# A third place in PSUM for the turned cross-attention exponents of a decoder layer

## What is computed

```
x = x + self_attn(layernorm(x))                 # 16 heads of 32: 6 plain, 4 hyperbolic, 6 cosine
x = x + cross_attn(layernorm(x), ctx)           # 16 heads, 224 queries, 750 keys per batch, mask
x = x + peer_ffn(layernorm(x))                  # product keys, 8 heads x top 8 of 128*128 experts

# cross_attn, per batch and head (d = 32):
att = (q @ k.T) / sqrt(d)                       # 224 x 750
att = att * mask - 1e10 * (1 - mask)
att = softmax(att)
out = att @ v                                   # 224 x 32, then @ Wo + bo
```

## Time and profile before

| what | value |
| --- | --- |
| median of 3 runs | 2667.64 us (2662.12, 3053.95, 2667.64) |
| the profiled execution's own time | 2672.23 us |
| its span, first to last instruction | 2670.4 us |
| PE busy | 2355.7 us, 88% |
| DVE busy | 1870.6 us, 70% |
| ACT busy | 1185.9 us, 44% |
| POOL busy | 1122.6 us, 42% |

### The profile page before, as it was taken

How to read it: one execution, slowest core, us unless ns; L and a number is a source line. 1 busy time by engine, 2 the same in 40 slices (tenths; PEclk the granted TensorE clock), 3 DMA queues, 4 the chain that set the end, 5 groups by cost and what they waited for, 6 DMA issues and landing times. The chain is left out here.

```text
span 2670.4 us, 37760 instructions
## 1 busy us (share of the span) xinstructions
PE 2355.7 (88%) x12440; PEld 1263.5 (47%) x12440; DVE 1870.6 (70%) x5466; ACT 1185.9 (44%) x3230; POOL 1122.6 (42%) x1084
## 2 busy tenths in 40 slices
PE   7899999999999999999777799898989898897777
PEld 3455564555655556555554344444444344443322
DVE  3477676776768667677554896878878787878555
ACT  1447365573745737466351343343334333433322
POOL 2121111211112111121001676777777777777775
PEclk9899999999999999999878899999999999999999
DMA  5000101001010010100202998999999999999998
GB/s 179 8 24 8 37 2 30 16 8 38 1 45 1 8 38 1 45 1 22 93 1 85 372 391 335 399 401 418 395 416 397 410 409 399 400 395 395 407 416 355
DMA packets 161362, 520.73 MB, mean 195 GB/s; under 512 B 17168, under 2 KB 27408, under 8 KB 161168
## 3 DMA queue, kind: packets, MB, share of 16 engines
q0 software_dynamic: 129024, 469.82, 44.3%
q1 hardware_dynamic: 30560, 46.98, 5.3%
q10 hardware_dynamic: 1584, 1.52, 0.2%
HBM read 507.71 MB, written 10.55 MB: 194 GB/s over the span
## 5 line engine op out<-in xcount | busy, mean ns | idle before, releaser
L1593 POOL DMA_INDIRECT e_rows<-in_experts,e_idx x896 | 888.2, 991 | 340.9 <-issue 287.7
L1650 PE MATMUL e_ps_out<-e_rows,e_diag 128*128 128x512 f32 x1792 | 843.5, 617 | 145.3 <-ACT e_diag L1917 145.1
L1811 DVE CUSTOM_DVE_ANT_0 e_rows<-e_rows,xn_all 128x512 f32<-128x512 f32 x896 | 567.8, 689 | 232.0 <-DMA e_rows<-in_experts,e_idx 231.8
L1650 PEld LDWEIGHTS e_ps_out<-e_rows,e_diag 128*128 128x128 f32 x1792 | 343.8, 197 | 594.3 <-issue 428.5
L1917 ACT ACTIVATE e_diag<-ident_f,e_weight 128x128 f32<-128x128 f32 x896 | 286.2, 390 | 313.1 <-DVE e_weight L1822 297.6
L984 DVE SCALAR_TENSOR_TENSOR ring<-ps_s,mask 112x750 f32<-112x750 f32 x256 | 232.8, 936 | 152.7 <-PE ps_s L557 115.2
L1170 ACT ACTIVATE ring<-ring,neg_max 112x750 f32<-112x750 f32 x256 | 233.4, 914 | 165.3 <-DVE neg_max L994 165.3
L568 PE MATMUL ps_t<-ident,ring 112*125 112x112 f32 x1536 | 233.6, 290 | 47.9 <-ACT prob_t L1188 36.5
L568 PEld LDWEIGHTS ps_t<-ident,ring 112*125 112x125 f32 x1536 | 199.7, 196 | 122.9 <-ACT ring L1170 61.7
L1912 ACT ACTIVATE e_active<-e_hidden 128x4 f32<-128x4 f32 x224 | 45.9, 205 | 456.4 <-DVE e_hidden L1811 456.2
L1188 ACT COPY prob_t<-ps_t 125x336 f32<-125x336 f32 x512 | 200.1, 440 | 95.6 <-PE ps_t L568 95.4
(11 more groups left out here) (186 smaller groups left out, 2850.4 us busy)
## 6 DMA issues: line engine op xcount, KB each, us to landing
e_rows<-in_experts,e_idx POOLq DMA_INDIRECT x896, 6.2
xn_t<-in_ctx_t SPq DMA_DIRECT2D x8, 1500.0 KB, 6.5
w_in<-in_ffn_wq SPq DMA_DIRECT2D x16, 256.0 KB, 6.2
acc<-in_x SPq DMA_DIRECT2D x8, 448.0 KB, 5.0
x_dram<-x SPq DMA_DIRECT2D x8, 448.0 KB, 3.1
acc<-x_dram SPq DMA_DIRECT2D x7, 512.0 KB, 6.1
out<-acc SPq DMA_DIRECT2D x14, 256.0 KB, 5.9
x2n_dram<-ring SPq DMA_DIRECT2D x7, 448.0 KB, 3.3
```

What stands on the lines that cost most here:

```text
L1593: pool.indirect_dma_start(rows[:, v % RING, k, :], None, table[:, :], bass.IndirectOffsetOnAxis(ap=idx[:, e:e + 1], axis=0))\
L1650: mm = nc.tensor.matmul(ps_out[t % 2][:], diag[:, HU * (v % ND) + k, :], rows[:, v % RING, k, D:], start=(s == 0 and k == 0), stop=(s == S ...
L1811: last = nc.vector.tensor_tensor_reduce(down, down, xn_all[:, t, :], 1.0, 0.0, ALU.mult, ALU.add, hidden[:, b, k:k + 1])
```

## The change

Sets of transposes get a third place: columns 112 to 447 of the bank `ps_o`, beside the 112 columns that the weighing uses. `turn_place` says which set goes where: in quad 0 the two places alternate as before; in the quads 1 to 7 the eight sets go to the places 0, 1, 2, 0, 1, 2, 0, 1, so that sets 2 and 5 of a quad (second unit, first set; third unit, second set) lie in `ps_o`. `turn_before` says which set held the place before: two sets back for the first two sets of a quad, three sets back for the others. Set 2 of a quad waits for `co_ready` of the quad before (the weighed outputs have been copied out of `ps_o`) in place of a `cpt_ready`. ACT's copy reads from the place that the set has. No instruction is added, and none changes its place in its stream. 14 of a batch's 64 sets lie in `ps_o`, 112 in the whole program.

```diff
+        turn_bank = (ps_t[0][:, 0:HB], ps_t[1][:, 0:HB], ps_o[:, TT:TT + HB])
+
+        def turn_place(n):
+
+            return n % 2 if n < 8 else (0, 1, 2, 0, 1, 2, 0, 1)[n % 8]
+
+        def turn_before(n):
+
+            return n - (2 if n < 8 or n % 8 < 2 else 3)
+
...
                 pe.wait_ge(cp_ready.sem, cp_ready.at(b, u + 1))
                 for i in range(2):
-                    if u >= 1:
-                        pe.wait_ge(cpt_ready.sem, cpt_ready.at(b, 2 * u - 1 + i))
+                    n = 2 * u + i
+                    out = turn_bank[turn_place(n)]
+                    if turn_place(n) == 2 and n % 8 == 2:
+                        pe.wait_ge(co_ready.sem, co_ready.at(b, u // 4))
+                    elif u >= 1:
+                        pe.wait_ge(cpt_ready.sem, cpt_ready.at(b, turn_before(n) + 1))
                     for j in range(3):
                         o = (3 * i + j) * CT
-                        mm = nc.tensor.transpose(ps_t[i][0:CT, j * TT:(j + 1) * TT], ring[:, u % NRING, o:o + CT],
+                        mm = nc.tensor.transpose(out[0:CT, j * TT:(j + 1) * TT], ring[:, u % NRING, o:o + CT],
                                                  ident[0:TT, 0:TT])
...
-                    nc.scalar.copy(prob_t[0:CT, u % 4, i * HB:(i + 1) * HB], ps_t[i][0:CT, 0:HB])\
+                    nc.scalar.copy(prob_t[0:CT, u % 4, i * HB:(i + 1) * HB], turn_bank[turn_place(2 * u + i)][0:CT, :])\
                         .then_inc(cpt_ready.sem, 1)
```

## The result

The changed kernel takes 2656.16 us (median of 15 runs, 2649.3 to 2661.2), the kernel before 2663.62 us (median of 15 runs of the same session): 7.5 us less. One run before, of 3053.95 us, is a slow one, and the ratio, 0.997 with a 95% interval of 0.996 to 0.998, is that of the fast runs. The profiled execution took 2661.2 us with a span of 2659.4, against 2672.23 and 2670.4 before. The feed-forward part is as long as it was: in the chain of waits its first large piece starts 11.5 us earlier than in the earlier trace rows,

A forecast was written before the change was run, and what follows sets the result against it. PE was taken to bound the batches, the loop from engine to engine the last cross stage. Gains of 3.1 + 1.6 = 4.7 us against the 2667.64 us median gave 2663 us, range 2650 to 2674.

The forecast's parts named there:

- the forecast's own case: Whole program: likeliest 2663 us, range 2657 to 2668, gains of 0 to 10 us, chance 0.62.
- The main mechanism: Attention's turning matmuls: waits on ACT's copies of sets nearly vanish, while waits on other things grow; 4.7 us gained.
- Iteration 2: In a batch: DVE's two masks run without waiting and swallow the 0.86 us of waiting ahead of the turns; gain 0.
- Iterations 5 and 6: In a batch: turning of q and k still waits for ACT's copy of `ps_y`; gain 0 in both.
- Iteration 7: In a batch: second unit's turn, DVE's mask and scores of half 1 move earlier; 0.34 us, bounded by 0 and 0.80.
- Middle stage: Quad 7 in a batch: ACT's order holds the weighing back, so only about 0.10 us comes through (0 to 0.19).
- Last stage: Last cross stage: nothing at the higher clock, 0.33 us in four lower-clock quads, 0.35 in the last quad; together 1.6 us.
- the sum for the batches: Iteration 7 plus Middle stage: 0.44 us a batch, times 7 = 3.1 us; between 0 and 27.3 us.
- the rival to which I gave 0.12: Last stage: PE keeps its higher clock in four quads, 7.5 us in place of 1.3; 2656.7 us, chance 0.12.
- the batches show no swings: Batches: clock swings appear only where PE idles over 1 us twice in a quad, and the batches show none.
- The costs taken at 0: Writing into and copying from the other bank's columns 112 to 447: taken as 0; costs' upper bound 2.9 us.
- The rival by which the clock falls in more quads than before: Last stage and batches: more quads fall to 1.2 GHz, 17 us lost against 4.7 won; 2680 us, chance 0.08.

The follow-up runs named there:

- e6_keys_after: Changed kernel with ACT's output of the keys' group 6 put behind quad 7's last two copies; batch 161.51 us, ratio to before 0.9974.
- e11_shifted: Changed kernel with twelve more unread identity transposes ahead of the last cross stage's first scores; 2665.5 us in a single run.
- e10: Changed kernel, but in the last batch only set 2 of a quad lies in `ps_o`; 2653.91 us in a single run.
- c_change_again: Changed kernel run again unedited as a control; 2656.27 us, ratio to before 0.9962.
- e2_batches_only: Changed kernel with the third place used only in batches 0 to 6, the last batch turning as before; ratio to before 0.9986.
- e3: Changed kernel with only set 2 of a quad in `ps_o`, set 5 staying in `ps_t`; ratio to before 0.9989.
- first four experiments: Changed kernel with third place in last batch only, in the other batches only, for set 2 alone, for set 5 alone; ratios 0.9976, 0.9986, 0.9989, 1.0.

## Why the prediction was right, and where its sizes were not

Forecast were 2663 us, a gain of 4.7 on the median shown; measured were 2656.16 us, a gain of 7.5, interval 5 to 11. The time lies within the range of 2650 to 2674 us, and 0.8 us below that of the forecast's own case (2657 to 2668). Of the 6.8 us between forecast and measurement 4.0 are the median before, which came out at 2663.62 over 15 runs in place of 2667.64 over three, and 2.8 are the gain. The main mechanism holds: the waits on copies of sets are nearly gone, and the next waiters keep most of the time. Part of the last stage's gain is luck, as told below. Compared from the markers (794.85 before, 463.44 after), event by event:

| Place | Gain forecast, us | Gain measured, us |
|---|---|---|
| Iteration 2 | 0 | 34.04 - 33.90 = 0.14 |
| Iterations 5 and 6 | 0 and 0 | 0.04 and 0.05 |
| Iteration 7 | 0.34 | 0.33 |
| Middle stage | 0.10 (0 to 0.19) | 0.21 |
| One batch | 0.44 | 0.79, with roundings |
| Seven batches | 3.1 | 5.5 |
| Last stage | 1.6 | 3.8 |

**Iteration 7** came out to 0.01 us. DVE in the change, and before it ACT:

```profile
549.85 2.03 DVE L998 SCALAR_TENSOR_TENSOR ring<-ps_s,mask 112x750 f32<-112x750 f32 x2 [1.36 <-PE ps_s L567]
```

```profile
549.58 0.23 ACT L1138 COPY q_t<-ps_o 128x112 f32<-128x112 f32 x1
549.71 0.77 ACT L1202 COPY prob_t<-ps_t 125x336 f32<-125x336 f32 x2
...
550.84 0.44 ACT L1202 COPY prob_t<-ps_o 125x336 f32<-125x336 f32 x1
```

The masks end at 551.88 and the scores start at 551.94. Whether a faster mask would free more was not tried.

**Iteration 2 was misread**, and this is the step of the sum for the batches that failed. I read one row, two masks in 1.91 us without waiting, as DVE at work throughout. But a row of x2 hides what lies between its two. The same two masks in the change:

```profile
495.52 1.77 DVE L998 SCALAR_TENSOR_TENSOR ring<-ps_s,mask 112x750 f32<-112x750 f32 x2
```

Two masks take 1.77 us, so before, the second had waited 0.14 us, for the second unit's turn. The rest of the 0.86 us was swallowed there as said: the scores now wait 0.52 us for DVE.

**Iterations 5 and 6** gave about 0.05 us each: the turning of q and k does wait for ACT's copy of `ps_y` (two waits, 0.5 us, in the waits above) and brings only what iteration 2 had won; the rest lies behind it, where the scores start 0.75 us after the third unit's turn in place of 0.80. Before, ACT's copy of the second unit's first set ended at 862.56 (in the batch of the marker at 794.85) and the third unit's turn started at 862.72, about one release later. So a short wait on that copy, too short to be listed, is likely what went; no run tests it.

**The middle stage** gave 0.21, past my upper end of 0.19 by 0.02. The third unit's exponent is bounded by DVE's reduction, as I took it: after the change the reduction ends at 561.69 + 0.08 = 561.77 and the exponent starts at 561.81. But I took 0.10 us for that release, and it took 0.04. e6_keys_after shows what else ACT's order behind it holds back: 0.50 us a batch.

**The last stage** was mis-sized because the clock stayed up in three more quads, the rival to which I gave 0.12. It came in for three of its four quads, and 2.0 us were given back at the two ends together: 3.8 us in all instead of 7.5. The working held at both levels. At the higher one quads stayed at 10.0 us. At the lower one two quads of e11_shifted took (1350.11 - 1326.99)/2 = 11.56 us each, against 11.88 before: 0.32 us won, forecast 0.33. What I had no ground for was to hold the clock's pattern fixed: e10 and e11 show that it changes where the rotation doesn't. The gain repeats (115.86 us in c_change_again), but no run shows the rotation to be its cause, so for this forecast what the last stage gained beyond 1.6 us is luck. The prediction was also wrong to say that the batches show no swings: its own trace has a marker of 8.01 us at 957.65, and the granted clock is 0.57 in its first 4 us.

**The costs taken at 0 were 0.** By form, ACT's copies out of `ps_o` and out of `ps_t` in the stretch 0 to 1400, and the turning matmuls into `ps_o`:

```profile
L1202 ACT COPY prob_t<-ps_o 125x336 f32<-125x336 f32 x112 | 49.8, 444 | 1.3 <-PE ps_o L582 0.4
...
L582 PE MATMUL ps_o<-ident,ring 112*125 112x112 f32 x336 | 61.0, 291 | 15.4 <-ACT q_t L1138 13.6 <-ACT prob_t L1202 1.1
```

444 against 442 ns, 291 against 286, no more than noise of the mix. The rival by which the clock falls in more quads than before is seen nowhere: even in e11_shifted it falls in three of five, before in four of five. Three banks held the clock better than two in the traces of after and before (116.12 against 119.95 us), and e11_shifted lost it with the same three. The Trainium skill, in the section that the prediction weighed (TensorE: Matmul & The Clock Gate, "A second HAM failure mode: psum-queue depth-cycling"), tells of a clock that swings where outputs are cycled through banks with small idle times between. Here the clock falls in the same quads with two banks (e2_batches_only, 121.77 us) as with three (e11_shifted, 119.86 us), so these runs don't bear out that the rotation makes it swing.

## What to carry to other kernels

A wait that ends on a scarce buffer is worth only the distance to the next waiter: of 27.3 us of waits in the batches 5.5 us were won, and the swallowing waits could be named in advance from the timelines of the other two engines. Where a merged row takes longer than its parts (1.91 us against 1.77), it holds a wait, and a claim that an engine was busy needs the single instructions. Measure small edits by periods between fixed markers inside one trace, and compare only periods with the same clock; here these repeat to 0.05 us, while whole runs spread by 12. Then look at the whole all the same: e6_keys_after won 0.50 us in each undisturbed batch and lost 3.2 us over seven, by falls of the clock elsewhere.

## What was not expected of the hardware

- The gap ahead of the q projection is 1.84 or 1.85 us in the batches shown, and the projection behind it runs in 6.32 us or in about 8.0 (in the last batch up to 9.0), in a changing pattern from run to run.
- In the last stage one and the same program took 117.29 and 120.12 us (set 2 alone, e10 and e3) and 119.95 and 121.77 us (two banks, before and e2); in the traces with set 2 in the third place the waits ahead of the turns are 1.20 us where the clock falls and where it holds. With 12 small extra matmuls at its start it took 120 in place of 116.
- The chip of the first four experiments runs this program 6% slower than the others, 2821 against 2664 us, and nearly all of it lies in the feed-forward part, which gathers the experts' rows: 1412 to 1425 against 1261 us. Undisturbed batches agree between them to 0.02 us.
